# One fused decoder layer on one core: the attention stage's first loads in another order, its rows of minus ones loaded instead of filled

## The chip, the cores and the metric

The kernel runs on one core of one Trainium2 chip. The metric is the device time of one execution in microseconds (us). Three runs of the kernel before gave 3306.53, 3310.98 and 3312.92 us, median 3310.98. The engines are TensorE (PE; its weight loads are shown as PEld), VectorE (DVE), ScalarE (ACT), GpSimd (POOL) and SyncE (SP). SP and ACT each issue DMA transfers here; the profile calls their issue lanes SPq and ACTq.

## The reference

A batch of 16 sequences of 256 rows by 512 channels goes through three stages, each with a residual and a layer norm: a state-space block, a cross attention and a feed-forward block with ternary weights. The change touches the attention, which works on the transposed view (256 channels, 512 positions, 16 heads of 16 channels):

```python
q = jnp.einsum('oc,bct->bot', Wq, target) + bq[None, :, None]
k = jnp.einsum('oc,bcs->bos', Wk, source) + bk[None, :, None]
v = jnp.einsum('oc,bcs->bos', Wv, source) + bv[None, :, None]
dot = jnp.einsum('bhdt,bhds->bhts', q, k) / math.sqrt(HEAD_DIM)
mask = target_mask[:, :, :, None] * source_mask[:, :, None, :]
dot = mask * dot - (1.0 - mask) * NEG
amap = jax.nn.softmax(dot, axis=-1) * mask
out = jnp.einsum('bhts,bhds->bhdt', amap, v)
```

## The kernel before, in words

The three stages run one after the other, each in a block of its own; every engine has its own written-out program in each, and semaphores order them. A block starts for all engines together.

**Scores.** q and k are split into three bf16 parts each, and six products of parts (`PAIRS`) stand for one f32 product. The parts are stacked along the partitions: for one head, 96 rows of `qst` or `kst` (6 pairs by 16 channels), then 6 rows that carry the mask in the same split form. The first score product (`scores_max`, L1276) contracts those 102 rows and gives the row maxima. The second (`scores_exp`, L1285) contracts 105: in the last 3 rows `qst` holds the three parts of each row's maximum and `kst` holds minus one, so that the maximum comes off within the product. The two buffers of a batch pair are `kst[:, 0]` and `kst[:, 1]`.

**Where the operands come from.** The stacks go through DRAM: q and k parts to `stack_d`, the mask rows of all 16 batches to `mask_d`, made once by POOL at the start of the state-space stage (L790 to L808) and stored by SP (L387). `load_group` (L1166) fetches 4 of the 16 heads: for each of the two operands one transfer of 96 rows from `stack_d` and one of 6 mask rows from `mask_d`, which counts 4 times 16 on `stack_in[g]`. The minus ones are not loaded: two fills by POOL (L1484, L1485) set all of `kst` to minus one once, before anything is loaded into it (`preset`).

**The loop.** The attention's body runs for b = -1 to 16 over units u = 0 to 15, one head each. In b = -1 the scores' maxima of batch 0 are taken, and beside them k, q of batch 1 and v of batch 0 are projected; the softmax of batch 0 starts in b = 0. Batch 0's stacks were made in the state-space stage. In unit u DVE takes the two row maxima of a head (L1557), which free the two PSUM buffers of `scores_max`; between them it takes over whatever projection PE finished (L1588, L1595). In u = 0 DVE also takes the statistics of batch 1's rows `x1r` (L1562 to L1567); POOL then forms their inverse root (`rs`, L1534), and in u = 2 DVE writes the normalised rows `x1n` (L1574), which q's projection reads. POOL waits, ahead of its whole body, for `params`: all of ACT's last four loads (`id2`, `wv_sb`, `w_sc`, `bv_sb`). k's projection needs ACT's first four (`ctx_sb` of batch 1, `wk_sb`, `wq_sb`, `qkb`).

After k and q of batch 1 are split (ACT L1426, POOL L1495 and L1497), SP stores the parts (L1164), loads the groups again, and moves the split maxima through `m_d` (L1183, L1186); `scores_exp` waits for those.

Of the kernel before, what the change touches and what calls it, by code (L numbers as in the profile page):

```python
# [5 lines left out]
F32 = mybir.dt.float32  # L6
BF16 = mybir.dt.bfloat16
ALU = mybir.AluOpType
# [4 lines left out]
BATCH, SEQ, HID = 16, 256, 512  # L13
# [126 lines left out]
def state_space_phase(nc, xT, x, w_in, w_bc, w_dt, w_dtproj, w_out, chan, ident, w_ffn, bc_scratch, w_scales, x1,  # L140
# [6 lines left out]
    with ExitStack() as ctx:  # L147
# [55 lines left out]
        mk_rows = bu[0:BATCH, 0:3].rearrange("b i c -> b (i c)").bitcast(BF16).rearrange("b (o r t) -> b o r t", o=2, r=len(PAIRS))  # L203
# [139 lines left out]
        def _(sp):  # L343
# [43 lines left out]
            sp.dma_start(mask_d.rearrange("(b k) -> b k", b=BATCH), mk_rows.rearrange("b o r t -> b (o r t)")).then_inc(mk_out, 16)  # L387
# [401 lines left out]
        def _(pool):  # L789
            pool.memset(w_sum[:, :], 0.0)  # L790
            pool.wait_ge(mk_in, 16)
            pool.tensor_scalar(mk_n, mk, 1.0, NEG, ALU.subtract, ALU.mult)
            for side, part in enumerate((mk, mk_n)):
                at = [[pair[side] for pair in PAIRS].index(i) for i in range(3)]
                pool.drain()
                pool.tensor_copy(mk_rows[:, side, at[0], :], part)
                pool.drain()
                pool.tensor_tensor(mk_r, part, mk_rows[:, side, at[0], :], ALU.subtract)
                pool.drain()
                pool.tensor_copy(mk_rows[:, side, at[1], :], mk_r)  # L800
                pool.drain()
                pool.tensor_tensor(mk_rows[:, side, at[2], :], mk_r, mk_rows[:, side, at[1], :], ALU.subtract)
                pool.drain()
                for r, pair in enumerate(PAIRS):
                    if r not in at:
                        pool.tensor_copy(mk_rows[:, side, r, :], mk_rows[:, side, at[pair[side]], :])
# [178 lines left out]
HG = 4  # L985
# [9 lines left out]
MINUS_ONES = -(1 + 0xBF80 * 2.0 ** -23)  # L995
# [14 lines left out]
def cross_attention_phase(nc, x1, ctxt, mask, maskT, wq, wk, wv, chan_qk, bv, ident, w_ffn, w_scales, stack_d, mask_d, m_d, x1n_d, w_tern, x2):  # L1010
# [5 lines left out]
    with ExitStack() as ctx:  # L1016
# [3 lines left out]
        def sem(name):  # L1020
            return ctx.enter_context(nc.semaphore(name))
# [60 lines left out]
        preset = sem("preset")  # L1082
# [59 lines left out]
        def _(sp):  # L1142
# [6 lines left out]
            def rows(a, b, size):  # L1149
                return a[bass.ds(b * size, size)]  # L1150
# [15 lines left out]
            def load_group(f, par, g, operands=(0, 1)):  # L1166
                m, h0 = g // 2, g % 2 * HG
                for opnd in operands:
                    st = (qst, kst)[opnd]
                    sp.dma_start(st[0:BLK, par, g * HG:(g + 1) * HG, :],  # L1170
                                 stack_d[opnd, m, :, h0:h0 + HG, :]).then_inc(stack_in[g], 16)
                    src = rows(mask_d, f * 2 + opnd, len(PAIRS) * HID).rearrange("(r o t) -> r o t", t=HID, o=1)
                    sp.dma_start(st[BLK:ROWS1, par, g * HG:(g + 1) * HG, :],
                                 src.to_broadcast([len(PAIRS), HG, HID])).then_inc(stack_in[g], 16)
# [14 lines left out]
            load_group(0, 0, 0, (0,))  # L1189
            load_group(0, 0, 1, (0,))  # L1190
            load_x1(1)
            sp.wait_ge(preset, 1)
            for g in range(2):
                load_group(0, 0, g, (1,))
# [3 lines left out]
            sp.wait_ge(preset, 2)  # L1198
# [67 lines left out]
        def _(pe):  # L1266
            pe.wait_ge(preset, 1)

# [123 lines left out]
        def _(act):  # L1392
# [13 lines left out]

            load_ctx(1, 1)
# [74 lines left out]
        def _(pool):  # L1482

            pool.memset(kst[:, 0].rearrange("p h t -> p (h t)").bitcast(F32), MINUS_ONES).then_inc(preset, 1)  # L1484
            pool.memset(kst[:, 1].rearrange("p h t -> p (h t)").bitcast(F32), MINUS_ONES).then_inc(preset, 1)  # L1485
# [489 lines left out]
def build(nc, ins, out):  # L1975

    def dram(name, shape, dt=F32):
        return nc.dram_tensor(name, shape, dt, kind="Internal").ap()
# [6 lines left out]
    mask_d = dram("mask_d", (BATCH * 2 * len(PAIRS) * HID,), BF16)  # L1985
# [52 lines left out]
```

## Time and profile before

| | |
|---|---|
| median of three runs | 3310.98 us |
| profiled execution, its own time | 3310.6 us |
| its span | 3308.8 us |
| state-space stage, about | 0 to 1836 us |
| attention stage, about | 1837 to 2900 us |
| feed-forward stage, about | 2900 to 3309 us |
| PE, DVE, ACT, POOL busy over the span | 92%, 84%, 73%, 63% |
| mean granted TensorE clock | 0.977 of full |

The shares of busy time are means over three stages and say little about one short stretch. The stretch that the change touches is the first 30 us of the attention stage, from 1837 us on, and about 1 us of POOL's work near the start of the program. The timeline gives the start and the busy time of each piece of work, and in square brackets how long its engine sat idle before it and what released it. A matmul of f32 is counted as two entries.

### The profile page before, as it was taken

Reading aid. Unit: us, or ns where it says so; the run is one execution under the profiler, and the core shown is the slowest. Engines: PE = TensorE matmul, PEld = TensorE weight load, DVE = VectorE, ACT = ScalarE, POOL = GpSimd, SP = SyncE. Lnnn points to the kernel's source line nnn. Section 1 sums busy time; section 2 is a strip of 40 time slices with the busy share of each in tenths; the row PEclk is TensorE's granted clock in tenths of the full one; section 3 lists DMA queues with packets and bytes.
Section 4 is the critical chain, followed back from the end, with each engine's and each line's share of the span. In section 5 each row is a group of like instructions: output and inputs, shape, how many; then the busy total and the mean of one; then the engine's idle time right before and its main releaser. Section 6 shows DMA issues by size and latency. Waiting matters only on the chain. (4 is left out here: it accounts for less than half of the span.)

```text
span 3308.8 us, 46151 instructions
## 1 busy us (share of the span) xinstructions
PE 3032.2 (92%) x16134; PEld 1825.8 (55%) x16134; DVE 2788.8 (84%) x2773; ACT 2409.6 (73%) x4531; POOL 2094.6 (63%) x1207
## 2 busy tenths in 40 slices
PE   7899999999999999999987699999999999879998
PEld 4677667766776677667755334444444443234444
DVE  6999999999999999999998677777787787278887
ACT  4877787778777877788786167767767767667776
POOL 5999999999999999999999234434434433200000
PEclk9999999999999999999998799999999999989999
DMA  4012201221122112211221555555555554131111
GB/s 169 30 45 77 77 33 55 77 77 36 52 77 77 43 46 77 77 44 44 77 93 64 162 155 161 176 175 167 178 167 173 172 170 128 47 118 46 45 45 36
DMA packets 164376, 311.86 MB, mean 94 GB/s; under 512 B 22736, under 2 KB 80208, under 8 KB 164000
## 3 DMA queue, kind: packets, MB, share of 16 engines
q1 hardware_dynamic: 158784, 299.53, 28.3%
q10 hardware_dynamic: 5360, 9.38, 0.9%
q8 instruction: 129, 2.11, 0.3%
q14 instruction: 103, 0.84, 0.1%
HBM read 217.16 MB, written 91.69 MB: 93 GB/s over the span
## 5 line engine op out<-in xcount | busy, mean ns | idle before, releaser
L820 POOL TENSOR_TENSOR bu<-du,bc 128x1024 f32<-128x1024 f32 x512 | 1197.3, 2363 | 82.0 <-DMA bc<-bc_scratch 63.4
L698 ACT ACTIVATE states<-dt,negA 128x256 f32<-128x256 f32 x2048 | 852.2, 463 | 360.3 <-DVE hc L917 335.3
L904 DVE TENSOR_TENSOR_SCAN states<-states,bu 128x1024 f32<-128x1024 f32 x352 | 805.9, 2289 | 73.8 <-ACT states L698 66.8
L1557 DVE TENSOR_REDUCE mmax<-s_ps 128x2 f32<-128x1024 f32 x512 | 624.7, 1224 | 204.3 <-PE s_ps L1276 185.5
L1401 ACT ACTIVATE pt<-s_ps 128x512 f32<-128x512 f32 x1024 | 573.4, 597 | 292.8 <-PE s_ps L1285 279.7
L917 DVE TENSOR_TENSOR hc<-states,bc 128x1024 f32<-128x1024 f32 x352 | 430.8, 1224 | 41.1 <-DVE states L904 6.4
L518 PE MATMUL y_ps<-id_sb,hc 128*128 128x128 f32 x2816 | 381.0, 279 | 81.6 <-DVE hc L917 81.6
L518 PEld LDWEIGHTS y_ps<-id_sb,hc 128*128 128x128 f32 x2816 | 324.8, 143 | 207.3 <-DVE hc L917 168.4
L1285 PE MATMUL s_ps<-qst,kst 105*128 105x512 bf16 x1024 | 378.7, 383 | 14.6 <-ACT pt L1401 5.1
L829 POOL TENSOR_TENSOR hp<-hp,bc 128x1024 f32<-128x1024 f32 x160 | 377.8, 2361 | 16.2 <-DVE hp L904 16.0
L904 DVE TENSOR_TENSOR_SCAN hp<-states,bu 128x1024 f32<-128x1024 f32 x160 | 364.7, 2279 | 6.0 <-ACT states L698 6.0
L1276 PE MATMUL s_ps<-kst,qst 102*128 102x512 bf16 x1024 | 315.0, 390 | 26.1 <-DMA kst<-mask_d 17.9
L1296 PE MATMUL pv_ps<-pt,vaug 128*32 128x512 f32 x2048 | 272.1, 604 | 21.9 <-ACT o_sb L1442 21.4
L483 PE MATMUL proj<-xpad,diagW 128*128 128x256 f32 x960 | 243.8, 384 | 35.7 <-ACT xpad L656 35.7
L478 PE MATMUL proj<-xT_sb,win_sb 128*128 128x256 f32 x1024 | 257.7, 390 | 14.9 <-DMA win_sb<-in_w_in 6.9
L480 PE MATMUL proj<-win_sb,xT_sb 128*128 128x512 f32 x512 | 242.3, 593 | 0.0
L1805 PE MATMUL gu_ps<-gu,xqT 128*128 128x512 bf16 x1024 | 234.6, 382 | 8.0 <-ACT xqT L1858 6.3
L495 PE MATMUL proj<-wout_sb,y 128*128 128x512 f32 x512 | 240.0, 598 | 0.9 <-ACT y L668 0.9
L1276 PEld LDWEIGHTS s_ps<-kst,qst 102*128 102x128 bf16 x1024 | 79.9, 98 | 267.6 <-DVE mmax L1557 193.0
L478 PEld LDWEIGHTS proj<-xT_sb,win_sb 128*128 128x128 f32 x1024 | 192.9, 197 | 39.6 <-issue 9.6
L483 PEld LDWEIGHTS proj<-xpad,diagW 128*128 128x128 f32 x960 | 173.2, 190 | 75.2 <-issue 56.6
L1285 PEld LDWEIGHTS s_ps<-qst,kst 105*128 105x128 bf16 x1024 | 99.2, 98 | 177.2 <-ACT pt L1401 104.7
(172 smaller groups left out, 4240.8 us busy)
## 6 DMA issues: line engine op xcount, KB each, us to landing
bc<-bc_scratch SPq DMA_DIRECT2D x128, 512.0 KB, 7.8
stack_d<-parts SPq DMA_DIRECT2D x180, 256.0 KB, 3.0
qst<-stack_d SPq DMA_DIRECT2D x64, 384.0 KB
kst<-stack_d SPq DMA_DIRECT2D x64, 384.0 KB
x<-xres SPq DMA_DIRECT2D x31, 512.0 KB, 5.2
w_raw<-in_w_ffn SPq DMA_DIRECT2D x48, 256.0 KB, 2.8
w_raw<-in_w_ffn SPq DMA_DIRECT2D x16, 768.0 KB, 7.2
xT_sb<-in_xT SPq DMA_DIRECT2D x16, 512.0 KB, 3.2
```

Of the source, the lines that this page charges most:

```text
L478: m = pe.matmul(proj[:, 0:SEQ], win_sb[:, k, 0, i * P:(i + 1) * P], xT_sb[:, k, :], start=start, stop=stop)
L483: m = pe.matmul(proj[:, 0:SEQ], diagW[:, i, k, :], xpad[:, i % 2, k:k + SEQ], start=start, stop=stop)
L518: m = pe.matmul(y_ps[:, i, :], src[:, n * SEQ + i * P:n * SEQ + (i + 1) * P], id_sb[:, :], start=False, stop=(c == CPT - 1 and n == NS - 1 ...
L698: a = act.activation(states[:, bank, first:first + SEQ], dt[:, t, :], ACT.Exp, scale=negA[:, t, c * NS + n:c * NS + n + 1])
L820: pool.tensor_tensor(bu[:, buf, :].rearrange("p (n l) -> p n l", n=NS), du[:, t % (2 * GRP):t % (2 * GRP) + 1, :].to_broadcast([P, NS, SEQ ...
L829: pool.tensor_tensor(h, h, bc[:, k % CPT, 1, :], ALU.mult).then_inc(hc_pool, 1)
L904: m = dve.tensor_tensor_scan(dst, src, bu[:, BU_OF[k][0], half * 2 * SEQ:(half + n) * 2 * SEQ], 0.0, ALU.mult, ALU.add)
L917: m = dve.tensor_tensor(hc[:, i % 2, cols], states[:, bank:bank + n, :].rearrange("p i l -> p (i l)"), bc[:, c, 1, cols], ALU.mult)
L1276: m = pe.matmul(s1_ps[:, pair, i, :], qst[0:ROWS1, par, u, tt * P:(tt + 1) * P], kst[0:ROWS1, par, u, :], start=True, stop=True)
L1285: pe.matmul(s2_ps[:, st % 2, :], kst[0:ROWS2, par, u, st * P:(st + 1) * P], qst[0:ROWS2, par, u, :], start=True, stop=True).then_inc(s2_re ...
L1401: act.activation(pt[:, g % 2, u % HG, st, :], s2_ps[:, st % 2], ACT.Exp).then_inc(exp_done, 1)
L1557: dve.tensor_reduce(mmax[:, u // HG, c:c + 2], s1_ps[:, pair], AX.X, ALU.max).then_inc(s1_free, 1)
```

## The change

1. `mask_d` gets 15 rows per batch instead of 12: the 6 rows of q, the 6 of k, then 3 rows of minus one, which one POOL fill of 16 partitions by 1536 bf16 elements writes beside the mask's rows. `mk_rows` takes four of the `bu` buffers instead of three.
2. `load_group` loads 9 rows instead of 6 behind the k stack, in every batch. The two fills of `kst`, their semaphore `preset`, and the waits for it on PE and SP are gone.
3. SP's first loads: group 0 for both operands, group 1 for both, then x1r, the mask, groups 2 and 3. Before, both q stacks and x1r went ahead of the k stacks.
4. ACT waits until group 0 has arrived (`stack_in[0]`, 4 times 16) before it issues its first load.

```diff
-        mk_rows = bu[0:BATCH, 0:3].rearrange("b i c -> b (i c)").bitcast(BF16).rearrange("b (o r t) -> b o r t", o=2, r=len(PAIRS))
+        mk_rows = bu[0:BATCH, 0:4].rearrange("b i c -> b (i c)").bitcast(BF16)[:, 0:MASK_ROWS * HID].rearrange("b (r t) -> b r t", t=HID)
...
             pool.tensor_scalar(mk_n, mk, 1.0, NEG, ALU.subtract, ALU.mult)
+            pool.memset(mk_rows[:, 2 * len(PAIRS):, :], -1.0)
...
-MINUS_ONES = -(1 + 0xBF80 * 2.0 ** -23)
+MASK_ROWS = 2 * len(PAIRS) + 3
...
-                    src = rows(mask_d, f * 2 + opnd, len(PAIRS) * HID).rearrange("(r o t) -> r o t", t=HID, o=1)
-                    sp.dma_start(st[BLK:ROWS1, par, g * HG:(g + 1) * HG, :],
-                                 src.to_broadcast([len(PAIRS), HG, HID])).then_inc(stack_in[g], 16)
+                    first, count = (f * MASK_ROWS + opnd * len(PAIRS)) * HID, (ROWS1, ROWS2)[opnd] - BLK
+                    src = mask_d[bass.ds(first, count * HID)].rearrange("(r o t) -> r o t", t=HID, o=1)
+                    sp.dma_start(st[BLK:BLK + count, par, g * HG:(g + 1) * HG, :],
+                                 src.to_broadcast([count, HG, HID])).then_inc(stack_in[g], 16)
...
-            load_group(0, 0, 0, (0,))
-            load_group(0, 0, 1, (0,))
+            load_group(0, 0, 0)
+            load_group(0, 0, 1)
             load_x1(1)
-            sp.wait_ge(preset, 1)
-            for g in range(2):
-                load_group(0, 0, g, (1,))
             load_mask(1)
             for g in range(2, HGROUPS):
                 load_group(0, 0, g)
-            sp.wait_ge(preset, 2)
...
         def _(pe):
-            pe.wait_ge(preset, 1)
-
...
+            act.wait_ge(stack_in[0], 4 * 16)
             load_ctx(1, 1)
...
-            pool.memset(kst[:, 0].rearrange("p h t -> p (h t)").bitcast(F32), MINUS_ONES).then_inc(preset, 1)
-            pool.memset(kst[:, 1].rearrange("p h t -> p (h t)").bitcast(F32), MINUS_ONES).then_inc(preset, 1)
             pool.memset(half_neg[:, :], -0.5)
             pool.wait_ge(params, 4 * 16)
```

SP at the start of the attention stage, before (`x1r` is the second batch's rows, `m_bc` its mask; 96x2048 is one stack of four heads):

```order
L1170 DMA qst<-stack_d 96x2048
L1173 DMA qst<-mask_d 6x4x512
L1170 DMA qst<-stack_d 96x2048
L1173 DMA qst<-mask_d 6x4x512
L1153 DMA x1r<-x 128x2x512
L1170 DMA kst<-stack_d 96x2048 [waits preset]
L1173 DMA kst<-mask_d 6x4x512
L1170 DMA kst<-stack_d 96x2048
L1173 DMA kst<-mask_d 6x4x512
L1156 DMA m_bc<-in_mask 128x512
```

The same place after the change:

```order
L1171 DMA qst<-stack_d 96x2048
L1175 DMA qst<-mask_d 6x4x512
L1171 DMA kst<-stack_d 96x2048
L1175 DMA kst<-mask_d 9x4x512
L1171 DMA qst<-stack_d 96x2048
L1175 DMA qst<-mask_d 6x4x512
L1171 DMA kst<-stack_d 96x2048
L1175 DMA kst<-mask_d 9x4x512
L1154 DMA x1r<-x 128x2x512
L1157 DMA m_bc<-in_mask 128x512
```

Group 0 is complete with the fourth transfer instead of the seventh; x1r moved from the fifth place to the ninth; nothing in the row waits any more.

ACT at its entry to the attention stage, after the change (before, the same rows without the wait; `parts<-kf` is ACT's first compute of the stage there):

```order
L1401 DMA ctx_sb<-in_ctx 128x2x512 [waits stack_in0]
L1406 DMA wk_sb<-in_wk 128x512
L1406 DMA wq_sb<-in_wq 128x512
L1406 DMA qkb<-in_qk_bias 128x4
L1401 DMA ctx_sb<-in_ctx 128x2x512
L1409 DMA id<-in_ident 128x128
L1409 DMA wv_sb<-in_wv 128x512
L1409 DMA w_sc<-w_scales 128x4
L1410 DMA bv_sb<-in_bv 128x256
L1423 ACTIVATE parts<-kf 128x1024 [waits k_ev]
```

All nine loads of ACT now stand behind the arrival of group 0; their order among themselves is kept, and `params` is still complete only with the last of them.

## Rows read from the trace of the kernel before

**Rows 1.** Timeline at the attention stage's start: start us, us, engine, line, work.
```profile
1837.04 3.51 POOL L1484 MEMSET kst<- 128x4096 f32 x1 [14.80 <-POOLq L147]
...
1837.07 0.45 ACTq L1405 DMA_DIRECT2D ctx_sb<-in_ctx  x1
...
1838.54 0.44 SPq L1153 DMA_DIRECT2D x1r<-x  x1
1838.54 0.77 ACTq L1409 DMA_DIRECT2D qkb<-in_qk_bias  x1
...
1840.58 0.31 SPq L1170 DMA_DIRECT2D kst<-stack_d  x1
...
1851.82 1.86 PE L1276 MATMUL s_ps<-kst,qst 102*128 102x512 bf16 x4 [17.95 <-DMA kst<-mask_d]
...
1856.11 2.77 PE L1361 MATMUL misc<-ctx_sb,wk_sb 128*128 128x256 f32 x6
```

**Rows 2.** Windows, 1837 to 1860 us: PE, PEld, DVE, ACT, POOL busy, PEclk, DMA share, GB/s.
```profile
1837.00:1839.00 2.00, 0.00 (x0) 0.00 (x0) 1.04 (x1) 1.28 (x1) 1.96 (x1) 0.50 0.40 102
1839.00:1841.00 2.00, 0.00 (x0) 0.00 (x0) 2.00 (x1) 0.00 (x0) 2.00 (x2) 0.50 0.83 226
1841.00:1860.00 19.00, 7.62 (x18) 3.70 (x19) 7.16 (x12) 0.00 (x0) 3.04 (x2) 0.50 1.06 271
```

**Rows 3.** DMA queues and issues, 1837 to 1863 us (SP's queue is q1, ACT's q10).
```profile
DMA packets 3104, 6.17 MB, mean 237 GB/s; under 512 B 608, under 2 KB 1056, under 8 KB 3104
q1 hardware_dynamic: 1552, 4.13, 61.8%
q10 hardware_dynamic: 1552, 2.04, 30.1%
x1r<-x SPq DMA_DIRECT2D x1, 512.0 KB, 10.1
qkb<-in_qk_bias ACTq DMA_DIRECT2D x1, 2.0 KB, 9.3
```

**Rows 4.** Timeline from 1862 us on, the chain through the normalised rows.
```profile
1862.06 1.21 DVE L1557 TENSOR_REDUCE mmax<-s_ps 128x2 f32<-128x1024 f32 x1
...
1862.27 0.70 POOL L1534 TENSOR_TENSOR rs<-ve,half_neg 128x2 f32<-128x2 f32 x1 [18.23 <-DMA bv_sb<-in_bv]
1863.19 0.99 DVE L1574 TENSOR_SCALAR x1n<-x1r,mv,rs 128x512 f32<-128x512 f32 x2
...
1865.42 0.74 DVE L1588 SCALAR_TENSOR_TENSOR kf<-misc,qkb,m_bc 128x512 f32<-128x512 f32 x1
...
1866.21 1.56 PE L1361 MATMUL misc<-x1n,wq_sb 128*128 128x256 f32 x6 [1.15 <-DVE kf L1588]
...
1870.18 1.56 PE L1361 MATMUL misc<-x1n,wq_sb 128*128 128x256 f32 x6 [1.11 <-DVE qf L1588]
...
1878.88 1.06 ACT L1426 ACTIVATE parts<-qf 128x1024 bf16<-128x1024 f32 x1 [8.33 <-DMA stack_d<-parts]
```

**Rows 5.** Timeline of POOL at the program's start.
```profile
16.99 1.73 POOL L806 COPY bu<-bu 16x512 bf16<-16x512 bf16 x3
46.06 2.35 POOL L820 TENSOR_TENSOR bu<-du,bc 128x1024 f32<-128x1024 f32 x1 [27.34 <-DMA bc<-bc_scratch]
```

**Rows 6.** Timeline, first issue of a later load of groups 0 and 1.
```profile
1891.62 0.33 SPq L1170 DMA_DIRECT2D qst<-stack_d  x1
```

**Rows 7.** Windows over that later load, by SP's queue alone.
```profile
1892.00:1896.00 4.00, 2.96 (x14) 1.89 (x13) 3.04 (x4) 0.91 (x2) 0.00 (x0) 1.00 0.71 207
1896.00:1901.00 5.00, 2.40 (x10) 0.43 (x7) 4.91 (x5) 1.33 (x4) 0.82 (x3) 1.00 1.05 247
```

**Rows 8.** Windows by TensorE's granted clock, 1851.8 to 1876 us.
```profile
1851.80:1860.40 8.60, 8.02 (x19) 3.81 (x20) 6.96 (x10) 0.00 (x0) 0.00 (x0) 0.50 1.05 251
1860.40:1876.00 15.60, 10.47 (x43) 5.83 (x41) 13.43 (x16) 2.11 (x2) 4.95 (x3) 0.99 0.41 133
```

**Rows 9.** Waits, 1900 to 2860 us: us in total, times, longest.
```profile
PE s_ps L1285 <- DMA qst<-m_d: 0.5, 1, 0.5
```

More of the change, by code:

```diff
@@ L386, in _ @@
             sp.wait_ge(mk_ready, 1)
-            sp.dma_start(mask_d.rearrange("(b k) -> b k", b=BATCH), mk_rows.rearrange("b o r t -> b (o r t)")).then_inc(mk_out, 16)
+            sp.dma_start(mask_d.rearrange("(b k) -> b k", b=BATCH), mk_rows.rearrange("b r t -> b (r t)")).then_inc(mk_out, 16)
             save_bc(0)
@@ L792, in _ @@
             pool.tensor_scalar(mk_n, mk, 1.0, NEG, ALU.subtract, ALU.mult)
+            pool.memset(mk_rows[:, 2 * len(PAIRS):, :], -1.0)
             for side, part in enumerate((mk, mk_n)):
+                rows = mk_rows[:, side * len(PAIRS):(side + 1) * len(PAIRS), :]
                 at = [[pair[side] for pair in PAIRS].index(i) for i in range(3)]
                 pool.drain()
-                pool.tensor_copy(mk_rows[:, side, at[0], :], part)
+                pool.tensor_copy(rows[:, at[0], :], part)
                 pool.drain()
-                pool.tensor_tensor(mk_r, part, mk_rows[:, side, at[0], :], ALU.subtract)
+                pool.tensor_tensor(mk_r, part, rows[:, at[0], :], ALU.subtract)
                 pool.drain()
-                pool.tensor_copy(mk_rows[:, side, at[1], :], mk_r)
+                pool.tensor_copy(rows[:, at[1], :], mk_r)
                 pool.drain()
-                pool.tensor_tensor(mk_rows[:, side, at[2], :], mk_r, mk_rows[:, side, at[1], :], ALU.subtract)
+                pool.tensor_tensor(rows[:, at[2], :], mk_r, rows[:, at[1], :], ALU.subtract)
                 pool.drain()
@@ L805, in _ @@
                     if r not in at:
-                        pool.tensor_copy(mk_rows[:, side, r, :], mk_rows[:, side, at[pair[side]], :])
+                        pool.tensor_copy(rows[:, r, :], rows[:, at[pair[side]], :])
             pool.drain()
@@ L1081, in cross_attention_phase @@
         m_in = [sem(f"m_in{g}") for g in range(HGROUPS)]
-        preset = sem("preset")
         vaug_set = sem("vaug_set")
@@ L1984, in build @@
     stack_d = dram("stack_d", (2, 2, BLK, 8, HID), BF16)
-    mask_d = dram("mask_d", (BATCH * 2 * len(PAIRS) * HID,), BF16)
+    mask_d = dram("mask_d", (BATCH * MASK_ROWS * HID,), BF16)
     x1n_d = dram("x1n_d", (BATCH * SEQ * HID,))
```

## The prediction

> **What bounds the kernel there.** I read the timeline of the attention stage's first 30 us first, then who waits for whom in it, then the windows with the share of the 16 DMA engines, and last the issues with their times to landing. The reader is to see four things.
>
> First, PE does nothing from the stage's start at 1837.04 until 1851.82, 14.8 us, and what ends that is the mask's transfer into `kst` of group 0 [rows 1]. SP had issued the first k stack only at 1840.58, after the POOL fill that ended at 1837.04 + 3.51 = 1840.55. That looks like the price of the fill and of the order of the loads, and it is what the change takes away.
>
> Second, the DMA engines are full in that time: share 0.83 from 1839 to 1841 and 1.06 from 1841 to 1860 [rows 2]. From 1837 to 1863, 6.17 MB move, 4.13 on SP's queue and 2.04 on ACT's, with as many packets on the one as on the other [rows 3]. So group 0 is late because it shares the engines with everything else.
>
> Third, there is a second gate behind the first. In unit 2 of b = -1 DVE writes x1n, at 1863.19 [rows 4]. It is in order on DVE, so no row maximum of unit 3 or later can pass it. It needs POOL's `rs`, which started at 1862.27 after 18.23 us of idle time ended by `bv_sb`, the last of ACT's loads (landed, by that, at about 1862.1). DVE's row maximum before it ran from 1862.06 to 1863.27. Both reasons thus end within 0.3 us of one another: DVE's own work, and the last landing of the whole prologue.
>
> Fourth, the stage's later work hangs on x1n and on k's second half right behind it (1865.42): both are followed by the splitting, the store of the parts, the loads of batch 1 and the maxima through DRAM. q's second half has room: the cast of q waits until 1878.88 for the store of k's parts [rows 4].
>
> **The change, part by part.** The sum is made against the profiled execution, 3310.6 us of its own for a span of 3308.8; that is 0.4 us below the median of the three runs.
>
> *The fill near the start.* One POOL fill on 16 partitions is added. Its nearest rows are the copies of 16x512 bf16, 1.73 us for three, and the 128x4096 fill, 3.51 us [rows 1, 5]. I take 1.7 us and bound it by 0.1 and 3.5. POOL ends the mask's work at 16.99 + 1.73 = 18.7 us and starts its next at 46.06, after 27.34 us idle [rows 5]. The mask's store, one quarter longer, has the same room. Cost 0. Without that cover it would be 1.7.
>
> *The two fills and the waits removed.* POOL loses 7.0 us; it has nothing else until `rs`, so by itself this gives nothing. SP's wait of 1.6 us (1838.54 + 0.44 to 1840.58) goes.
>
> *Group 0 alone.* A later load of two groups by SP with no other queue at work shows what to expect: issued at 1891.62, it moved 207 GB/s from 1892 to 1896, 0.83 MB [rows 6, 7]. One group is 2 x 384 KB and 48 mask rows of 1 KB, 0.835 MB, now 0.85. So group 0 takes about 4.6 us and lands at 1841.7 instead of 1851.8. PE starts 10 us earlier. This is the visible part of the change.
>
> *What is late next, first.* PE then needs only the first row maxima for its eight products of units 0 and 1, and stands before k's projection. That needs ACT's first four loads. Before, they were issued from 1837.07 and the fourth had landed at 1838.54 + 9.3 = 1847.8, 10.8 us later [rows 1, 3]. Now they start at 1841.7, and the same 10.8 us give 1852.5; since x1r and the groups behind compete, up to 1854.5. DVE at the same time stands before x1r's statistics in unit 0: x1r took 10.1 us in fifth place and is now ninth, about 1849 to 1850.5. k's projection starts near 1853.5 instead of 1856.1, so DVE reaches x1n some 1 to 2.5 us before 1863.2, and not 10.
>
> *What is late next, second.* x1n still waits for `bv_sb`, the last of ACT's nine loads, and these now start 4.7 us later. The queues share the engines packet by packet (1552 and 1552 [rows 3]), and all bytes that had to move still have to: 6.17 MB plus 48 rows of 1 KB, 0.05 MB, which at 247 GB/s [rows 7] is 0.2 us. What was wasted at the start grows: while SP's queue is alone the share is 0.71 for the first 4 us [rows 7] where it was 0.83 and soon 1.06 [rows 2]. With about 0.88 as the mean of the old first 4 us that is 4 x 0.17 / 1.06 = 0.65 us. So the last landing goes from 1862.1 to about 1863.0, and now ACT's queue surely is the last to end, since SP's remaining loads had a start. x1n moves with it: +0.9 us. The bounds are -1.3 (DVE's own work ends first and the loads come no later than 1860.8) and +3 (ACT's small packets served alone at the end at the 0.71 share).
>
> A rule of the Trainium skill speaks against the change in the same way: "DMA: Bandwidth & Descriptors", section "Issuing engines are not separate DMA queues", says that transfers started by different engines run on the same 16 engines and interleave. By it, holding ACT's loads back makes group 0 early and the rest as much later; the trace agrees, with 1.06 of the engines' time in use while both queues were open [rows 2].
>
> *PE's clock.* Before, PE ran at 0.50 of the clock (1.2 GHz) from 1851.8 to 1860.4 while busy 8.02 of 8.60 us, then at 0.99 (2.4 GHz) until 1876 [rows 8]. The projection's first six entries took 2.77 us at the low level and 1.56 at the high one [rows 1, 4]. After the change PE is busy for some 4 us from 1841.8, idle until 1853.5, and busy again. Its clock may therefore rise later, when q is projected. Each of q's two projections at the low level costs 1.2 us and a little more for the scores between. I take one of them: +1.2. The bounds are 0 and 5.7: three units of 4.0 us each (1866.21 to 1870.18 [rows 4]), each longer by those 1.2 and, as an estimate, 0.7 for its two other entries and four score products.
>
> The Trainium skill bears on this in "TensorE: Matmul & The Clock Gate", section "HAM oscillation — how this bites in real kernels": waits for DMA between short bursts of matmuls let the clock fall. By it the low level would hold through much of 1853 to 1865; here row by row the clock did rise only after a nearly full stretch [rows 8].
>
> *Nine rows instead of six in every group.* 12 packets of 1 KB per group at 247 GB/s are 0.05 us, 3.2 us over 64 groups if all were on the path. Between 1900 and 2860 PE waited for the maxima's transfer behind them once, 0.5 us [rows 9]. Cost 0, bound 3.2. SP issues as many transfers as before.
>
> *Sum.* 0 (fill) + 0 (early PE, hidden behind x1n) + 0.9 (last landing) + 1.2 (clock) = +2.1 us: 3310.6 + 2.1 = 3312.7 us.
>
> **The rivals.** (A) The whole stage moves with PE's start. For it: PE's wait of 17.95 us is the longest of the stretch, and it goes. Price: -10, 3300.6 us. Against it: `bv_sb` would have to land by 1852, 6.2 MB in 15 us or 410 GB/s, where the windows show 226 to 271 [rows 2]. A gain of over 0.2% needs it by 1855.5. I give this 5%.
>
> (B) Slower: the clock. If PE stays at 1.2 GHz from 1861 to about 1875, k's second half and both halves of q are each 1.9 us longer, 5.7 in all; DVE's row maxima wait with them. With the +0.9 this gives +6.6, 3317.2 us; together with a last landing later than 1863 it passes 0.2%. It decides from the point where PE's busy stretch before 1863 is too thin to raise the clock. For it, the 7 us of idle time put in before k's projection; against it, q's room up to 1878.88 [rows 4], which hides part. 9%.
>
> (C) The extra rows sit on the path in each batch: +3.2 beside the rest, 3315.9 us. Against it: PE hardly waited for what stands behind these loads [rows 9]. 3%.
>
> (D) The forecast: the early start is given back at x1n, and the time stays where it was. 83%.
>
> **How the numbers follow.** The change can be told from none if it is over about 0.2%, 6.6 us; the three runs of before span 6.4 us. The forecast's own range is 3310.6 - 1.3 to 3310.6 + 3 + 3.6, or 3309 to 3317. With the spread of the runs, 3.2 us to either side at most, and part of B, I give 3306 to 3318. Faster by over 0.2% has nearly all of A and a tail of D's noise, 6%; slower has most of B, a little of C and the noise, 12%; the rest, 82%, is within 0.2%.
>
> **What would show it right or wrong.** In the profile of the changed kernel PE's first L1276 product should start near 1842; then PE and DVE should be idle for most of 1846 to 1853; DVE should be idle just before x1n with POOL's `rs` released by `bv_sb`, and x1n should start at 1863.5 to 1865 where it was 1863.19. `scores_exp` (L1285) should start within 3 us of 1904. The granted clock between 1861 and 1876 decides term two. If x1n starts before 1861, the argument on the bytes is wrong; if the stage's end moves while x1n does not, the path I followed from x1n is not the one that counts.

## The result and the profile after

The kernel after took 3316.76 us (median of 17 runs, 3312.67 to 3324.18) against 3312.39 us for the kernel before (median of 17, 3306.53 to 3316.67). The ratio is 1.0014, 95% interval 1.0008 to 1.0021: slower by some 4.4 us. That is less than the 0.2% taken here for no change, and with this many runs it is still told from none.

The profiled execution of after took 3324.18 us for a span of 3322.4, the longest of its runs. Of the 13.6 us between the two spans, 7.0 lie before the attention stage, which starts at 1844.06 where it was 1837.04. In the other kernels below that stage starts anywhere from 1835.05 to 1841.6, so most of this belongs to the execution. Landmarks are therefore counted from the attention stage's own start, T.

The first rows are after's timeline, with the columns of [rows 1].
```profile
1844.06 0.32 SPq L1171 DMA_DIRECT2D qst<-stack_d  x1
...
1850.59 0.42 ACTq L1401 DMA_DIRECT2D ctx_sb<-in_ctx  x1
1850.62 1.89 PE L1272 MATMUL s_ps<-kst,qst 102*128 102x512 bf16 x4 [10.53 <-DMA kst<-mask_d]
...
1852.04 0.51 ACTq L1406 DMA_DIRECT2D qkb<-in_qk_bias  x1
...
1867.70 2.93 PE L1357 MATMUL misc<-ctx_sb,wk_sb 128*128 128x256 f32 x6 [12.56 <-DMA qkb<-in_qk_bias]
...
1870.50 0.70 POOL L1528 TENSOR_TENSOR rs<-ve,half_neg 128x2 f32<-128x2 f32 x1 [26.34 <-DMA bv_sb<-in_bv]
1871.50 1.22 DVE L1551 TENSOR_REDUCE mmax<-s_ps 128x2 f32<-128x1024 f32 x1 [11.33 <-PE s_ps L1272]
1873.80 1.22 DVE L1551 TENSOR_REDUCE mmax<-s_ps 128x2 f32<-128x1024 f32 x1
...
1873.94 1.56 PE L1357 MATMUL misc<-ctx_sb,wk_sb 128*128 128x256 f32 x6 [1.61 <-DVE kf L1582]
...
1874.93 0.99 DVE L1568 TENSOR_SCALAR x1n<-x1r,mv,rs 128x512 f32<-128x512 f32 x2
...
1877.95 1.56 PE L1357 MATMUL misc<-x1n,wq_sb 128*128 128x256 f32 x6 [1.15 <-DVE kf L1582]
...
1915.56 1.04 PE L1281 MATMUL s_ps<-qst,kst 105*128 105x512 bf16 x2 [0.78 <-DMA qst<-m_d]
```
Set against [rows 1, 4], from T: PE's first score product starts at +6.56 (before +14.78), k's projection at +23.64 (+19.07), POOL's `rs` at +26.44 (+25.23), x1n at +30.87 (+26.15). The first `scores_exp` starts at +71.50 where it was +67.01, and PE's first work of the feed-forward stage (`tra_ps`) at +1075.6 where it was +1072.2. So the early start is there, and 4.7 us are lost by x1n; 4.5 of them are left at `scores_exp` and 3.4 at the end of the attention stage. From there to the end of the span this execution took 402.8 us against 399.6, in a stage that the change does not touch.

The waits of after, in total, times and longest, between 1836 and 1885 us:
```profile
POOL rs L1528 <- DMA bv_sb<-in_bv: 26.3, 1, 26.3
PE misc L1357 <- DMA qkb<-in_qk_bias: 12.6, 1, 12.6
PE s_ps L1272 <- DMA kst<-mask_d: 10.5, 1, 10.5
```
The longest of them is not the one that set x1n. `rs` was written at 1871.2, and DVE then still took two row maxima before x1n. It had been idle for 11.33 us before the first, for scores that stand behind k's projection on PE. The 12.6 us wait is the gate.

Why `qkb` came so late is in the queues and the issues of after. The queue rows give packets, MB and the packets' time as a share of 16 engines, here for 1850.6 to 1854, then 1854 to 1856, then 1856 to 1860:
```profile
q1 hardware_dynamic: 404, 0.85, 102.5%
...
q1 hardware_dynamic: 237, 0.56, 101.8%
q10 hardware_dynamic: 23, 0.05, 12.6%
...
q1 hardware_dynamic: 208, 0.64, 59.5%
q10 hardware_dynamic: 210, 0.43, 40.8%
```
Issues of after, 1840 to 1866 us, with the time from issue to landing last:
```profile
wk_sb<-in_wk ACTq DMA_DIRECT2D x1, 256.0 KB, 13.1
...
bv_sb<-in_bv ACTq DMA_DIRECT2D x1, 128.0 KB, 15.8
qkb<-in_qk_bias ACTq DMA_DIRECT2D x1, 2.0 KB, 15.6
```
ACT issued from 1850.59 on, when SP had already issued 15 of its 18 loads. For the 3.4 us that followed ACT's queue moved no packet at all while SP's had the engines full; in the next 2 us it moved 23 against 237. Part of that silence is always there: ACT's first packet came 4.7 us after its first issue here, and 2.5 us after it in the kernel before. But in the kernel before both queues were issued at the same time, and ACT's then had the larger share. This is before's queue row, 1839 to 1843 (2 to 6 us from T):
```profile
q10 hardware_dynamic: 405, 0.78, 61.2%
q1 hardware_dynamic: 126, 0.35, 34.4%
```
SP's 1.6 us stop at the fill is not what gave ACT this lead. e2 below has neither the fill nor SP's wait, and its row for the same stretch from T, 1840.4 to 1844.4, is alike:
```profile
q10 hardware_dynamic: 409, 0.78, 60.2%
q1 hardware_dynamic: 121, 0.33, 31.9%
```
What takes the lead away is that SP's loads stand ahead of ACT's. `qkb`, 2 KB, then takes 15.6 us where it took 9.3 [rows 3].

The Trainium skill ("DMA: Bandwidth & Descriptors", section "Queues, rings and completion order") says that an engine goes round-robin between the queues with work for it, packet by packet. The equal counts of [rows 3] and the 208 and 210 packets above agree. The 405 against 126 and the 404 to none do not, unless one queue's packets were not yet there to choose from; no run here tells which it was.

### The profile page after: what moved, and what is told of

The parts are those of the page before. It is cut to its first block and busy times, and to the rows that moved or that the text cites. A ratio compares the mean times of both kernels' runs of the same rounds, so it can differ in the third digit from the quotient of the medians.

```text
span 3322.4 us, 46115 instructions
## 1 busy us (share of the span) xinstructions
PE 3028.4 (91%) x16101; PEld 1825.4 (55%) x16134; DVE 2790.3 (84%) x2773; ACT 2408.4 (72%) x4531; POOL 2087.4 (63%) x1206
## 5 line engine op out<-in xcount | busy, mean ns | idle before, releaser
L1799 PE MATMUL gu_ps<-gu,xqT 128*128 128x512 bf16 x993 | 227.7, 382 | 15.7 <-ACT xqT L1852 13.2
L478 PEld LDWEIGHTS proj<-xT_sb,win_sb 128*128 128x128 f32 x1024 | 191.9, 196 | 40.2 <-issue 9.9
```

What stands on the lines that cost most here:

```text
L478: m = pe.matmul(proj[:, 0:SEQ], win_sb[:, k, 0, i * P:(i + 1) * P], xT_sb[:, k, :], start=start, stop=stop)
L1799: mm = pe.matmul(gu_ps[:, c % 2, side, :], xqT[:, slot % 2, k, :], gu[:, c, side, k, :], start=(k == 0), stop=(k == HK - 1))
```

## The experiments

Each kernel is after with the edit shown, unless it says otherwise. The table gathers all: landmarks in us from T, and the time as ratio to before. Front is the first convolution of the program (DVE `u<-xpad`), in us from the span's start.

| kernel | first score | k's projection | `rs` | x1n | `scores_exp` | front | ratio, 95% |
|---|---|---|---|---|---|---|---|
| before | 14.78 | 19.07 | 25.23 | 26.15 | 67.01 | 20.28 | 1 |
| after | 6.56 | 23.64 | 26.44 | 30.87 | 71.50 | 21.34 | 1.0014 (1.0008 to 1.0021) |
| e1, no ACT wait | 9.93 | 14.24 | 24.55 | 25.29 | 67.29 | 22.25 | 1.0002 (0.9993 to 1.0011) |
| e2, rows alone | 15.28 | 19.59 | 24.63 | 26.68 | 67.58 | 21.45 | 1.0004 (0.9995 to 1.0012) |
| e3, `params` late | 6.38 | 24.23 | 13.59 | 31.07 | 71.29 | 21.43 | 1.0014 (1.0005 to 1.0022) |
| e4, first four free | 9.84 | 14.15 | 26.07 | 26.81 | 68.44 | 21.39 | 1.0013 (1.0004 to 1.0021) |
| e5, short queue | 10.01 | 14.32 | 15.28 | 21.41 | 62.03 | 21.36 | 0.9989 (0.9980 to 0.9998) |
| e6, e3 and e4 | 9.75 | 14.07 | 16.85 | 22.74 | 65.34 | 21.38 | 1.0001 (0.9992 to 1.0010) |
| e7, e1 and e3 | 9.73 | 14.05 | 18.61 | 24.50 | 66.52 | 21.45 | 1.0008 (1.0000 to 1.0017) |
| e8, before with the wait | 11.64 | 24.75 | 27.28 | 31.99 | 74.19 | 20.30 | 1.0016 (1.0007 to 1.0024) |
| e9, fill early | 6.47 | 23.68 | 26.33 | 30.73 | 71.74 | 20.51 | 1.0011 (1.0002 to 1.0019) |
| e10, e5 and e9 | 9.96 | 14.27 | 15.23 | 21.12 | 63.80 | 20.34 | 0.9985 (0.9976 to 0.9994) |
| e11, one queue | 6.70 | 11.01 | 11.97 | 17.86 | 59.93 | 20.34 | 0.9987 (0.9978 to 0.9996) |
| e12, with the fills | 13.06 | 17.35 | 18.31 | 24.20 | 66.03 | 20.34 | 0.9995 (0.9986 to 1.0004) |

**e1: ACT doesn't wait.**
```diff
-            act.wait_ge(stack_in[0], 4 * 16)
```


> The changed kernel with ACT's wait for group 0 taken out; the rest of the change stays. Counted from the attention stage's start, the kernel before began k's projection at +19.1 us and x1n at +26.2, the changed kernel at +23.6 and +30.9. Theory A (the loss is ACT's first four loads landing late, because they are held back): k's projection at +16 to +19, x1n back at +26 to +27, time within 1.5 us of the kernel before. Theory B (x1n follows the last landing, which follows the bytes): x1n at +26.3, the same time as A, so this run does not part A and B. Theory C (the extra rows and the fill cost 3 us or more over all batches): time still 3 us above the kernel before, whatever x1n does.

Measured: x1n at +25.29, the time that of before. k's projection comes earlier than was expected (+14.24) and is not the gate: x1n stands 0.7 us behind `rs`, which waits for `bv_sb`:
```profile
1852.35 2.77 PE L1357 MATMUL misc<-ctx_sb,wk_sb 128*128 128x256 f32 x6
...
1862.66 0.70 POOL L1527 TENSOR_TENSOR rs<-ve,half_neg 128x2 f32<-128x2 f32 x1 [24.45 <-DMA bv_sb<-in_bv]
```
The wait's removal takes the loss away. PE still starts 4.9 us earlier than before, and in time nothing comes of it. The front of this execution, 22.25, is no effect of the edit: DVE's whole row there began 0.9 us later than after's.

**e2: the rows alone.** The order of the loads is that of before, ACT doesn't wait, and the loaded rows of minus ones stay.
```diff
-            load_group(0, 0, 0)
-            load_group(0, 0, 1)
+            load_group(0, 0, 0, (0,))
+            load_group(0, 0, 1, (0,))
             load_x1(1)
+            for g in range(2):
+                load_group(0, 0, g, (1,))
...
-            act.wait_ge(stack_in[0], 4 * 16)
```


> The kernel before with one part of the change alone: the rows of minus one are loaded (nine rows behind k, the fill of 16x1536 at the start), the two fills of kst and the waits for them are gone; SP's order of loads is that of before and ACT does not wait. Theories A and B: time within 1.5 us of the kernel before; since SP no longer waits 1.6 us for the fill, group 0 may arrive about 1 us earlier, and x1n at +25.5 to +26.5. Theory C: 3 us or more slower than before.

Measured: all landmarks of the attention stage within 0.6 us of before, the front 1.2 us later, and the interval holds 1. Taking out the two fills and the `preset` wait gained nothing by itself. For the nine rows the interval alone is too wide, since it reaches 4.0 us; but from the first `scores_exp` to PE's first work of the feed-forward stage the kernels with nine rows took 1004.1 to 1005.9 us and the three with six rows (before, e8, e12) 1004.8 to 1005.2. Nine rows cost nothing there that shows.

**e3: POOL's wait for `params` moves to the first use of the ternary scales, so that `rs` is free of `bv_sb`.**
```diff
-            pool.wait_ge(params, 4 * 16)
...
+                    if batch == 0:
+                        pool.wait_ge(params, 4 * 16)
```


> The changed kernel with POOL's wait for ACT's last four loads moved from the head of its body to the first use of w_sc, so that rs needs only DVE's variance. Theory A: rs runs early, near +14, and x1n stays at +30 to +31, because k's projection stands before it; time within 1 us of the changed kernel, 4 us above the one before. Theory B: x1n comes 4 us or more earlier, and the time falls by that.

Measured: `rs` 12.9 us earlier, x1n where it was, and the time that of after.
```profile
1849.50 0.70 POOL L1529 TENSOR_TENSOR rs<-ve,half_neg 128x2 f32<-128x2 f32 x1 [13.49 <-DVE ve L1562]
...
1860.14 2.93 PE L1357 MATMUL misc<-ctx_sb,wk_sb 128*128 128x256 f32 x6 [13.32 <-DMA qkb<-in_qk_bias]
...
1866.98 0.99 DVE L1569 TENSOR_SCALAR x1n<-x1r,mv,rs 128x512 f32<-128x512 f32 x2
```
The theory that the last landing sets x1n in after is refuted: x1n starts 6.8 us behind k's projection with `rs` out of the way.

**e4: ACT's first four loads go free, the other five wait for group 0.**
```diff
-            act.wait_ge(stack_in[0], 4 * 16)
             load_ctx(1, 1)
             for dst, src in ((wk_sb, wk), (wq_sb, wq), (qkb, chan_qk)):
                 act.dma_start(dst.ap(), src).then_inc(kq_params, 16)
+            act.wait_ge(stack_in[0], 4 * 16)
```


> The changed kernel with ACT's wait moved behind its first four loads (ctx of batch 1, wk, wq, qkb), so that only the last five are held back until group 0 is there. Theory A: k's projection at +12 to +17, x1n at +26.5 to +27.5, now gated by rs and the last landing; time 3 to 4 us below the changed kernel and within 1.5 of the one before. Theory B: x1n at the last landing, +26.4 to +27.5, as the changed kernel's last landing is, so the same. Were neither right, x1n would stay at +31.

Measured: k's projection back at +14.15, x1n at +26.81, now again 0.7 us behind `rs`:
```profile
1854.12 2.77 PE L1357 MATMUL misc<-ctx_sb,wk_sb 128*128 128x256 f32 x6
...
1866.04 0.70 POOL L1528 TENSOR_TENSOR rs<-ve,half_neg 128x2 f32<-128x2 f32 x1 [25.97 <-DMA bv_sb<-in_bv]
```
x1n thus has two gates so far: k's projection plus some 7 us, and `bv_sb` plus some 1 us. The time did not come back with x1n as was expected: the ratio, 1.0013, is 1.8 us above what the landmarks say, which its interval covers.

**e5: neither gate, and little ahead in the queue.** e1 and e3 together, and SP issues group 0, x1r and the mask, and the other groups only when k's operands are there.
```diff
             load_group(0, 0, 0)
-            load_group(0, 0, 1)
             load_x1(1)
             load_mask(1)
-            for g in range(2, HGROUPS):
+            sp.wait_ge(kq_params, 3 * 16)
+            for g in range(1, HGROUPS):
                 load_group(0, 0, g)
```


> A version meant to beat both: the changed kernel without ACT's wait, POOL's wait for ACT's last four loads moved to the first use of w_sc, and SP holding groups 1 to 3 back until ACT's first four loads are there (SP: group 0, x1r, mask, then the wait, then groups 1 to 3). About 2.7 MB are needed before x1n instead of 6.2. If x1n's two gates (k's projection and the last landing) are the whole story: first score at +7 to +9, k's projection at +10 to +12, x1n at +14 to +17 where it was +26.2; the first scores_exp then 8 to 10 us earlier than +67.0, time 3302 to 3305. If what follows x1n has its own bound (DVE's 32 row maxima and the evacuations, some 47 us), scores_exp comes no earlier than about +58 and the gain is at most 9. If group 1 is late for unit 4, the gain shrinks by that.

Measured: x1n at +21.41, 4.7 us earlier than before, `scores_exp` 5.0 us earlier, and the ratio 0.9989, 3.6 us.
```profile
1851.14 1.89 PE L1272 MATMUL s_ps<-kst,qst 102*128 102x512 bf16 x4 [13.17 <-DMA kst<-mask_d]
...
1862.54 0.99 DVE L1568 TENSOR_SCALAR x1n<-x1r,mv,rs 128x512 f32<-128x512 f32 x2
...
1903.16 1.03 PE L1281 MATMUL s_ps<-qst,kst 105*128 105x512 bf16 x2 [0.76 <-DMA qst<-m_d]
```
PE starts 3.4 us later here than in after and the kernel is faster, so PE's start by itself decides nothing. The gain is under what was expected, because with both gates off the first score becomes the gate again: x1n stands 11.4 us behind it here, as it did in the kernel before (26.15 - 14.78).

**e6: both gates off (e3 and e4), SP's queue as in after.**
```diff
-            act.wait_ge(stack_in[0], 4 * 16)
             load_ctx(1, 1)
...
+            act.wait_ge(stack_in[0], 4 * 16)
...
-            pool.wait_ge(params, 4 * 16)
...
+                    if batch == 0:
+                        pool.wait_ge(params, 4 * 16)
```

> The changed kernel with both edits that took one gate each: first four loads of ACT ahead of its wait, and POOL's wait for the last four moved to the first use of w_sc. One alone gave x1n at +26.8 (gated by rs at +26.1), the other +31.1 (gated by k's projection at +24.2). If these are the two gates, both together give k's projection at +14 and x1n at +17 to +20, scores_exp at +59 to +62 (67.0 before), time 5 to 8 us below the kernel before. If a third gate stands close behind, x1n moves by less; x1r's statistics were at +14.6 and are no candidate before +17.

Measured: x1n at +22.74, but `scores_exp` at +65.34, only 1.7 us earlier than before, and no gain in time. All three expectations, x1n, `scores_exp` and the time, were missed. x1n now meets a third gate, x1r, ninth in SP's queue: its statistics end on DVE with `mv` at +16.28, and x1n starts 6.5 us behind that, as it does in e7. Of the 3.4 us won at x1n, half is lost behind it. k's second half is on the low clock, and so is the whole of the stretch; the window row (columns as in [rows 2]) is of 1863 to 1868 us.
```profile
1863.34 2.92 PE L1357 MATMUL misc<-ctx_sb,wk_sb 128*128 128x256 f32 x6 [1.87 <-DVE kf L1583]
```
```profile
1863.00:1868.00 5.00, 4.66 (x11) 3.12 (x12) 3.17 (x5) 0.00 (x0) 0.00 (x0) 0.50 1.03 275
```

**e7: e1 and e3, SP's queue as in after.**
```diff
-            act.wait_ge(stack_in[0], 4 * 16)
...
-            pool.wait_ge(params, 4 * 16)
...
+                    if batch == 0:
+                        pool.wait_ge(params, 4 * 16)
```

> The changed kernel without ACT's wait and with POOL's wait moved: all loads issued at once. x1n should be gated by x1r's statistics (at +16.8 when ACT did not wait) and the four row maxima of units 1 and 2 behind them: +21 to +23. scores_exp at +62 to +64, time 2 to 5 us below the kernel before, and 1 to 4 above the version that frees only the first four loads.

Measured: x1n at +24.50, later than expected, because x1r, ninth in SP's queue, comes last now (its statistics at +16.67 where they were at +13.35 in e5), and `rs` with it. The difference to e5 is SP's queue alone: 3.1 us of x1n. The time was expected below that of before and is not. The ratio, 1.0008, is worse than e5's by 0.0019 or 6.3 us, where `scores_exp` is 4.5 us later.

**e8: the kernel before with ACT's wait and nothing else of the change.**
```diff
+            act.wait_ge(stack_in[0], 4 * 16)
             load_ctx(1, 1)
```


> The kernel before with only ACT's wait for group 0 added; fills, order and rows as before. If the wait is what costs, and not the new order: group 0 lands at +9 to +11, ACT's first four loads 13 to 17 us after that, k's projection at +24 to +27, x1n at +31 to +34, scores_exp 5 to 8 us later than +67.0, time 5 to 8 us above the kernel before. If the wait costs only in the new order, where SP's whole row stands ahead of it, time stays within 1.5 us.

Measured: `scores_exp` 7.2 us later, ratio 1.0016.
```profile
1864.09 2.93 PE L1361 MATMUL misc<-ctx_sb,wk_sb 128*128 128x256 f32 x6 [8.61 <-DMA qkb<-in_qk_bias]
```
The wait alone, in the old order, with the old fills, costs as much as the whole change or more. With e1 this settles the cause from both sides.

**e9 and e10: the fill near the program's start moves ahead of the wait for the mask; e9 in after, e10 in e5.**
```diff
+            pool.memset(mk_rows[:, 2 * len(PAIRS):, :], -1.0)
             pool.wait_ge(mk_in, 16)
...
-            pool.memset(mk_rows[:, 2 * len(PAIRS):, :], -1.0)
```


> The changed kernel with one edit: POOL's fill of the three rows stands ahead of its wait for the mask instead of behind the mask's first operation. In the changed kernel DVE's first convolution starts at 21.34 us, in the kernel before at 20.28, and beside the fill one of DVE's 128x128 scalings took 1.47 us instead of 0.27. If the fill slows DVE while the two overlap (contention), moving it into POOL's idle time before 4.7 us, when DVE scales nothing yet, brings the first convolution back to 20.2 to 20.5. If the later start comes from something else in the change, it stays at 21.3. x1n and the first scores_exp stay at +31 and +71.5. Time about 1 us below the changed kernel, too little for the times alone.

> The short-queue version (no wait on ACT, POOL's wait moved, SP's groups 1 to 3 held until ACT's first four loads are there) with the fill moved ahead of the mask's wait as well. Convolution at 20.3 instead of 21.4, x1n at +21.4 and scores_exp at +62 as in the short-queue version; time 4 to 5 us below the kernel before (short queue alone: 3.4 below).

Measured: the first convolution comes at 20.51 in e9, whose diagonals also start 0.23 us later than after's, and at 20.34 in e10, against 21.34 in after and 20.28 before. First POOL's timeline of after, then that of e9:
```profile
6.85 1.42 POOL L793 MEMSET bu<- 16x1536 bf16 x1
...
18.45 1.72 POOL L808 COPY bu<-bu 16x512 bf16<-16x512 bf16 x3
```
```profile
0.75 1.37 POOL L791 MEMSET bu<- 16x1536 bf16 x1
...
17.22 1.73 POOL L808 COPY bu<-bu 16x512 bf16<-16x512 bf16 x3
```
DVE forms its diagonals beside that work. The same places of DVE in before, then in after:
```profile
6.86 0.27 DVE L872 TENSOR_SCALAR diagD<-id_sb,chan_sb 128x128 f32<-128x128 f32 x1
...
17.06 1.93 DVE L871 TENSOR_SCALAR diagW<-id_sb,chan_sb 128x128 f32<-128x128 f32 x4
18.91 0.27 DVE L872 TENSOR_SCALAR diagD<-id_sb,chan_sb 128x128 f32<-128x128 f32 x1
...
20.28 0.41 DVE L880 TENSOR_SCALAR u<-xpad,chan_sb 128x256 f32<-128x256 f32 x1
```
```profile
6.88 1.47 DVE L874 TENSOR_SCALAR diagD<-id_sb,chan_sb 128x128 f32<-128x128 f32 x1
...
17.23 2.46 DVE L873 TENSOR_SCALAR diagW<-id_sb,chan_sb 128x128 f32<-128x128 f32 x4
19.62 0.64 DVE L874 TENSOR_SCALAR diagD<-id_sb,chan_sb 128x128 f32<-128x128 f32 x1
...
21.34 0.41 DVE L882 TENSOR_SCALAR u<-xpad,chan_sb 128x256 f32<-128x256 f32 x1
```
A scaling that took 0.27 us in before took 1.47 us beside the fill of 1.42 us (the kernel before has such cases too, beside POOL's other work: 0.63 and 1.18 us), and the later ones are slowed until POOL is through, at 20.17 us (18.45 + 1.72) instead of 18.72. So the fill costs DVE 1.06 us, by contention and not by a wait. The Trainium skill ("SBUF — State Buffer", section "SBUF: two separate sides") says that a VectorE operation in a two-port mode and a GpSimd operation share one pair of ports, which the one that starts first holds for its whole instruction while the other is blocked. The two records, which end within 0.1 us of each other (6.88 + 1.47 and 6.85 + 1.42), agree; whether these scalings ran in such a mode no view of the trace shows. In time neither e9 against after nor e10 against e5 is told apart: 1 us is less than the intervals.

**e11: e10 with k's operands issued by SP, ahead of the mask.** ACT issues its other five loads when those are there.
```diff
+            sp.dma_start(ctx_sb[:, 1], first).then_inc(ctx1_in, 16)
+            for dst, src in ((wk_sb, wk), (wq_sb, wq), (qkb, chan_qk)):
+                sp.dma_start(dst.ap(), src).then_inc(kq_params, 16)
...
-            load_ctx(1, 1)
-            for dst, src in ((wk_sb, wk), (wq_sb, wq), (qkb, chan_qk)):
-                act.dma_start(dst.ap(), src).then_inc(kq_params, 16)
+            act.wait_ge(kq_params, 3 * 16)
```


> As the last, but all that is needed before x1n is on SP's queue in the order of use: group 0, x1r, ctx of batch 1, wk, wq, qkb, mask; ACT issues its other five loads, and SP groups 1 to 3, once those are there. If what counts is the order in which a byte is served, group 0 lands at +6.5 (alone) instead of +10, x1r at +9 to +10, k's projection starts at +11.5 to +13 instead of +14.3, x1n at +18.5 to +20, scores_exp at +59 to +60.5, time 6 to 8 us below the kernel before. If TensorE's clock stays at its low level for k's second half because of the gap between the first scores and k's projection, x1n is 1.5 us later than that.

Measured: the earliest landmarks of all, x1n at +17.86 and `scores_exp` at +59.93, 7.1 us before the kernel before.
```profile
1844.86 1.89 PE L1276 MATMUL s_ps<-kst,qst 102*128 102x512 bf16 x4 [9.88 <-DMA kst<-mask_d]
...
1849.17 2.77 PE L1361 MATMUL misc<-ctx_sb,wk_sb 128*128 128x256 f32 x6
1850.13 0.70 POOL L1530 TENSOR_TENSOR rs<-ve,half_neg 128x2 f32<-128x2 f32 x1 [11.87 <-DVE ve L1563]
...
1855.02 2.67 PE L1361 MATMUL misc<-ctx_sb,wk_sb 128*128 128x256 f32 x6 [1.74 <-DVE kf L1584]
1856.02 0.99 DVE L1570 TENSOR_SCALAR x1n<-x1r,mv,rs 128x512 f32<-128x512 f32 x2
```
Group 0 lands as early as in after (+6.70) and k's operands do not pay for it: no DMA wait stands before k's projection. What the change was to bring at these landmarks is to be had with one queue in the order of use. x1n stands 11.2 us behind the first score here and in e10, so the 3.3 us between the two are those of group 0's arrival. The gain in time is less than the 6 to 8 us expected. The time, 3306.91 us (0.9987), and e10's, 3307.15 us (0.9985), are the lowest of all and not told apart.

**e12: the fills kept, the old rows, and SP's short queue.** The edit is to the kernel before, with POOL's wait for `params` late as in e3. The order is not quite that of e5: since k's stack has to wait for the fill, x1r and the mask go ahead of it.
```diff
             load_group(0, 0, 0, (0,))
-            load_group(0, 0, 1, (0,))
             load_x1(1)
+            load_mask(1)
             sp.wait_ge(preset, 1)
-            for g in range(2):
-                load_group(0, 0, g, (1,))
-            load_mask(1)
-            for g in range(2, HGROUPS):
+            load_group(0, 0, 0, (1,))
+            sp.wait_ge(kq_params, 3 * 16)
+            for g in range(1, HGROUPS):
                 load_group(0, 0, g)
```

> The short queue without the loaded rows: the kernel before, its two fills of kst kept, with SP's order q of group 0, x1r, mask, wait for the fill, k of group 0, wait for ACT's first four loads, groups 1 to 3, and POOL's wait moved. Tells whether the loaded rows are needed for the gain. Theory: the fill ends at +3.5 while the queues are busy anyway, so group 0 lands 1 to 2 us later than the short queue's +10.0, x1n at +21.5 to +24, scores_exp at +62 to +64; the convolution starts at 20.3. Time 2 to 5 us below the kernel before. If the fill is a real delay, x1n is 3.5 us later than +21.4.

Measured: x1n at +24.20, 3.1 us later than in e10, `scores_exp` at +66.03 and later than expected, ratio 0.9995. The first score is 3.1 us later too (k's stack was issued 3.5 us from T), and x1n again stands 11.1 us behind it. So the loaded rows are worth those 3 us at x1n, by letting k's stack go early, once the rest of the queue is in order, and nothing in the old order (e2). In time e12 and e10 are not told apart.

**All together.** The time follows `scores_exp` and the front. Adding the two shifts against before, and beside them (ratio - 1) x 3312.5 us: after +5.6 and +4.6, e1 +2.3 and +0.7, e2 +1.7 and +1.3, e3 +5.4 and +4.6, e4 +2.5 and +4.3, e5 -3.9 and -3.6, e6 -0.6 and +0.3, e7 +0.7 and +2.6, e8 +7.2 and +5.3, e9 +5.0 and +3.6, e10 -3.2 and -5.0, e11 -7.0 and -4.3, e12 -0.9 and -1.7. The largest miss is 2.7 us, where the interval of such a ratio reaches 3.0 us to either side, and the landmarks are of a single execution. Whether any of e4's, e7's and e11's misses is real was not found. The feed-forward stage, which no kernel here changes, took 402.1, 405.3 and 403.4 us in these three executions where it took 399.6 in before, so a miss of this size can come from there.

x1n itself comes out of four gates, and the last one rules: the first score plus 11.1 to 11.4 us (before, e2, e5, e10, e11, e12), k's operands, that is k's projection plus some 7 us (after, e3, e8, e9), `rs` behind `bv_sb` plus 0.7 us (e1, e4), and x1r's `mv` plus 6.5 us (e6, e7).

## Why the prediction was right or wrong

The forecast of +2.1 us, no change, with 3306 to 3318 as the range, met +4.4: the range and the sign hold, and the claim that the early start is given back at x1n is what the traces show. That the total came so near is partly luck, since three terms missed and two of them, the clock and the fill, offset each other; and x1n was late for another reason than the one forecast.

Of the signs it named, the two that count failed: x1n came at T + 30.9 and not T + 26.5 to 28, and `scores_exp` 4.5 us later and not within 3. A third failed in part: `rs` was released by `bv_sb`, but DVE was not idle just before x1n.

*Group 0 alone.* PE starting 10 us earlier was off: 8.2 us. Group 0 landed 6.5 us after its issue and not 4.6. The 207 GB/s of [rows 7] are of a window that opens 0.4 us after the first issue of a later load; here the first 4 us moved 171, 0.68 MB (first row; the second is for the clock, below; columns as in [rows 2]):
```profile
1844.00:1848.00 4.00, 0.00 (x0) 0.00 (x0) 3.01 (x1) 1.28 (x1) 0.10 (x1) 0.50 0.53 171
...
1872.00:1888.00 16.00, 10.13 (x42) 5.71 (x40) 13.83 (x16) 2.11 (x2) 4.25 (x2) 1.00 0.37 119
```
Even so the 0.85 MB of group 0 alone would have been through by about 4.7 us, as an estimate from 0.68 MB in the first 4 us and the 245 GB/s of 1848.0 to 1850.6. By the time it landed 1.32 MB had moved, so some 0.47 MB of the loads issued behind it went in between; sizing the landing by group 0's bytes alone left that out. ACT's loads therefore began 6.5 us late and not 4.7.

*What is late next, first.* This step failed. It took the 10.8 us that ACT's first four loads had needed before and moved them to the new start, with k's projection near +16.5. They needed 17.1 us from the first issue (1850.59 to 1867.70), and k's projection came at +23.64. The 10.8 us were those of a queue issued at the same time as SP's; the wait put it behind SP's backlog of groups 1 to 3, x1r and the mask instead. The new order alone has a smaller share in it: in e1 and e4, where the four are issued at T, `qkb` landed at +12.9. "1 to 2.5 us before 1863.2" for DVE's side of x1n became 4.7 us after it. e1, e3, e4 and e8 show it: without the other gate x1n stays where it is (e3), with this one removed x1n falls back to the other (e1, e4; the time came back in e1, and in e4 that is not shown), and the wait alone brings the loss into the old kernel (e8).

*What is late next, second.* Right in itself, and no longer the term that counts. The forecast moved the last landing by +0.9; `rs`, released by it, moved by +1.2 (25.23 to 26.44), inside the bounds. The mistake was to hold this for the only gate that could rule: it bounds the end of the loads, and says nothing of which of them comes last among those that k needs.

*PE's clock.* Priced +1.2 at q's projections, measured about 0 there: both ran in 1.56 us, the high level's time, as did k's second half. k's first half took 2.93 us, the low level's time (2.77 before [rows 1]), and the granted clock was at 1.00 from 1872 on. It did show in eight of the twelve variants (e1, e4, e6, e7, e8, e10, e11, e12), where k's second half took 2.64 to 2.93 us; why there and not in the others was not found. e10 and e5 have x1n within 0.3 us of each other and `scores_exp` 1.8 us apart, and k's second half at 2.93 and 1.56 us. All 14 traces divide in the same way: from x1n to `scores_exp` it was 40.2 to 41.0 us in the six with k's second half at 1.56 us, and 41.6 to 42.7 us in the other eight. No run changed the clock by itself, so that it is the cause is argued, and well supported, but not shown.

*The fill near the start.* The duration was well taken (1.42 us within 0.1 and 3.5), the cover was not: POOL's idle time hides the fill from POOL, not from DVE beside it. It cost 1.1 us at the first convolution and not 0; that these reach the end of the program is not shown.

*Nine rows, and the fills removed.* Right, by e2 and the length of the stage behind `scores_exp` given there. PE's wait for the maxima's transfer is 0.8 us once, where it was 0.5 [rows 9].

*The sum as measured.* x1n +4.7, of which `scores_exp` keeps 4.5; the clock's term 0; the fill +1.1; together +5.6 against +4.4 in time, whose interval reaches from 2.6 to 7.0. Rival A fell: PE's start moved 8.2 us and the stage did not. B and C did not occur. No rival held that k's operands would come later than before by more than the wait itself; that case was missing.

## What to carry to other kernels

When loads are held back behind others, the bytes fix only when the last transfer lands. Which transfer is last is set by what the other queue has already put ahead. So recount the operands of every consumer against that backlog, and not against the latency that they had when both queues started together.

The longest wait of a stretch is not its price. Here x1n had four gates, and bringing the first score 4.9 us forward (e1) gained nothing that the time shows; list the gates and their distances before moving any.

Put what is needed first into the queues in the order of use, and hold the bulk back until it has landed (e5, e10, and e11 with one queue), rather than holding back what the next consumer needs (after, e8).

## What the runs showed of the hardware

A queue whose first transfer is issued behind another queue's backlog starts late and slowly. ACT's first packet came 2.4 to 2.6 us after its first issue in the ten kernels in which nothing stood ahead, and 4.7 to 5.3 us after it in the four in which SP's backlog did (after, e3, e8, e9). From 2 to 6 us after that issue its queue moved 32 to 55 packets in those four, against 305 to 473 of SP's; in the nine in which both queues were issued together it moved 384 to 424, against 118 to 167. In after 2 KB then took 15.6 us, and the 256 KB of `wk_sb` took 13.1.

A small GpSimd fill on 16 partitions beside VectorE's scalings stretched one of them from 0.27 to 1.47 us, and made the whole row end 1.1 us later, though neither engine waited for the other by any semaphore. In e9 and e10, where the fill ran before those scalings, none was stretched by it.
